# Second attention: outputs turned in 32x32 squares and divided by VectorE, score buffers fixed by head pair, a longer first table piece

## The reference

```python
proj = x @ w_in                                    # x: layer norm of the residual stream
k, v, q = split(proj, 3)                           # 16 heads of 16
scores = einsum('bhqd,bhkd->bhqk', q, k) / 4 + bias[:, q, k]   # bias depends on k - q alone
attn = einsum('bhqk,bhkd->bhqd', softmax(scores), v)
gated = attn.transpose(0, 2, 1, 3).reshape(b, s, 256) @ w_gate + b_gate
a, g = split(gated, 2)
x = x + a * sigmoid(g)
x = x + (fp8(layernorm(x)) @ w8.T + b8)
```

## Time and profile before

| | us |
|---|---|
| median of 3 runs | 2232.6 (2231.52 to 2234.2) |
| the profiled execution | 2231.65, its span 2229.9 |
| second attention, first bias sum to last division | 1567.6 to 2113.4 |
| close | 2115.8 to the end |
| mean granted TensorE clock | 0.949 |

### The profile page before, as it was taken

One profiled execution on the slowest core, in us unless ns is written; L12 is line 12 of the kernel. 1 busy time (PEld: TensorE's weight loads), 2 busy tenths in 40 slices (PEclk: granted clock), 3 DMA queues, 4 the chain that ended last, 5 costly groups with the idle time before them and its releaser, 6 DMA issues. The chain is left out here.

```text
span 2229.9 us, 38265 instructions
## 1 busy us (share of the span) xinstructions
PE 1991.4 (89%) x12467; PEld 1148.6 (52%) x12467; DVE 1164.6 (52%) x2132; ACT 1406.8 (63%) x1605; POOL 754.4 (34%) x643
## 2 busy tenths in 40 slices
PE   6899999999945799999999999778688888888797
PEld 5722333333332588888888888667122222222255
DVE  5511252524468434333333333375788888888666
ACT  5599999999732323233323332255699999999744
POOL 2000000001010423244244324110477777878622
PEclk9999999999955799999999999889799999999999
DMA  6744443435001421122022112188425343443011
GB/s 208 221 89 67 86 86 59 84 58 114 10 31 39 198 88 71 45 86 83 28 86 86 45 68 81 69 290 288 106 35 135 55 110 58 60 124 52 10 78 67
DMA packets 76840, 203.67 MB, mean 91 GB/s; under 512 B 13028, under 2 KB 28134, under 8 KB 74536
## 3 DMA queue, kind: packets, MB, share of 16 engines
q1 hardware_dynamic: 66920, 179.22, 30.4%
q0 software_dynamic: 6816, 18.62, 2.5%
q10 hardware_dynamic: 2896, 3.16, 0.5%
HBM read 338.84 MB, written 60.03 MB: 179 GB/s over the span
## 5 line engine op out<-in xcount | busy, mean ns | idle before, releaser
L1200 PE MATMUL psum<-A_qa,A_ka 50*128 50x512 f32 x2048 | 413.8, 468 | 72.5 <-ACT A1f_probs L1246 39.6
L1200 PEld LDWEIGHTS psum<-A_qa,A_ka 50*128 50x128 f32 x2048 | 170.1, 186 | 511.6 <-ACT A1f_probs L1246 257.5
L2328 PE MATMUL psum<-e_w_high,e_xT 128*128 x1136 | 386.1, 401 | 3.9 <-DVE e_xT L2278 3.8
L1358 POOL TENSOR_TENSOR A1f_probs<-A1f_probs,A1f_bias 128x512 f32<-128x512 f32 x256 | 326.3, 1285 | 154.5 <-ACT A1f_probs L1246 154.4
L1286 DVE SCALAR_TENSOR_TENSOR A1f_probs<-psum,A1f_bias 128x1024 f32<-128x1024 f32 x256 | 312.8, 1222 | 67.2 <-PE psum L1200 55.7
L1234 ACT ACTIVATE A0f_probs<-psum 128x1024 f32<-128x1024 f32 x256 | 307.8, 1202 | 23.5 <-PE psum L1200 22.2
L1246 ACT ACTIVATE A0f_probs<-psum 128x1024 f32<-128x1024 f32 x256 | 309.2, 1208 | 0.5 <-PE psum L1200 0.5
L2285 DVE TENSOR_TENSOR e_hT<-psum,e_hT 128x1024 fp32r<-128x1024 f32 x71 | 86.9, 1224 | 420.2 <-ACT e_hT L2249 420.2
L1238 ACT ACTIVATE A1f_probs<-A1f_probs 128x1024 f32<-128x1024 f32 x256 | 270.6, 1057 | 49.5 <-DVE A1f_probs L1286 49.4
L1216 PE MATMUL psum<-A1f_probs,v 128*32 128x512 f32 x2048 | 274.5, 607 | 3.7 <-POOL A1f_probs L1358 1.8
L1216 PE MATMUL psum<-A0f_probs,v 128*32 128x512 f32 x2048 | 275.0, 610 | 0.0
(11 more groups left out here) (283 smaller groups left out, 2601.0 us busy)
## 6 DMA issues: line engine op xcount, KB each, us to landing
e_w_raw<-in_experts SPq DMA_DIRECT2D x73, 3072.0 KB, 10.7
qk_parts<-L_part SPq DMA_DIRECT2D x64, 512.0 KB, 3.7
A_qa<-qk_parts SPq DMA_DIRECT2D x192, 128.0 KB, 4.3
A_ka<-qk_parts SPq DMA_DIRECT2D x192, 128.0 KB, 6.6
om<-results SPq DMA_DIRECT2D x16, 512.0 KB, 7.0
A1f_bias<-tables SPq DMA_DIRECT2D x32, 256.0 KB, 11.3
A1f_bias<-tables SPq DMA_DIRECT2D x16, 448.0 KB, 10.6
L_x<-in_x SPq DMA_DIRECT2D x8, 512.0 KB, 6.9
```

The lines of the kernel that those rows point to most:

```text
L1200: mm = e.matmul(ps[:, side * HALF:(side + 1) * HALF], self.qk.ka[rows, s, pair, kt * P:(kt + 1) * P].bitcast(FP32R), self.qk.qa[rows, s, p ...
L1358: e.tensor_tensor(fourth, fourth, self.bias_of(*w[1:], slice(self.FOURTH, GH)).rearrange("p h q -> p (h q)"), ALU.mult).then_inc(self.mult ...
L2328: mm = e.matmul(out, left[part].bitcast(FP32R), moving.bitcast(FP32R), start=start and i == 0, stop=stop and i == 2)
```

## The change

It does five things, all in the second attention and its close:

1. The block's outputs are no longer moved and turned by TensorE. `square` (VectorE) transposes a half's 128x512 sums from PSUM in 32x32 squares into `squares` and makes 16 reciprocals for each partition. `divide` (VectorE) multiplies 128x256 out of `squares`; for odd g a second 128x512 transpose in squares then puts two groups' outputs into `omT`, features in partitions. `move`, `finish` and their semaphores are gone.
2. One such piece is taken from a queue at each of the four `BY_POOL` steps of a block.
3. `BY_POOL` is now (0, 1), (0, 3), (1, 5), (1, 7), before it was (0, 0), (0, 2), (1, 4), (1, 6).
4. `score0` has a PSUM buffer of its own (one), `score1` has two. `score0` of step n waits for L1286 of step n-1, `score1` of step n for the exponential of step n-2.
5. The `FIRST` table piece has 768 columns instead of 512, and the others are waited for at (0, 3). The close reads `omT` in place of `f_omT`: its turns by TensorE and moves by ScalarE are gone, and w_gate's rows are laid out on the host in the turned order.

```diff
-    BY_POOL, THIRD_FROM, THIRD_TO = ((0, 0), (0, 2), (1, 4), (1, 6)), S - HALF, S + 2 * P
+    BY_POOL, THIRD_FROM, THIRD_TO = ((0, 1), (0, 3), (1, 5), (1, 7)), S - HALF + P, S + 3 * P
-    FIRST, OTHERS = ((S - HALF, S),), ((S, 2 * S - P), (0, S - HALF))
+    EARLY = 3
+    FIRST, OTHERS = ((S - HALF, S + (EARLY - 1) * P),), ((S + (EARLY - 1) * P, 2 * S - P), (0, S - HALF))
...
-            emptied = {"score0": self.biased[0], "score1": self.exped[1], "finish": self.normalised}
-        self.ring = Slots(3, [w for w in self.work if w[0] in emptied], emptied)
+            self.rings = [Slots(i + 1, [w for w in self.work if w[0] == kind], {kind: emptied})
+                          for i, (kind, emptied) in enumerate((("score0", self.biased[0]), ("score1", self.exped[1])))]
...
             if kt == BT - 1:
-                work.append(("move", at, half))
-                if half:
-                    todo.append(at)
+                out.extend((("square", at, half), ("divide", at, half)))
...
-                    if todo and kt == 4:
-                        work.append(("finish", todo.pop(0)))
+                    if out and (half, kt) in self.BY_POOL:
+                        work.append(out.pop(0))
...
+    def square(self, e, at, half):
+        steps = self.m.dve
+        self.wait_products(e, at, half)
+        e.wait_ge(steps.sem, steps.n)
+        e.transpose(self.squares[:, :], self.outputs(at, half)).then_inc(self.moved[half], 1)
+        e.wait_ge(self.moved[half], at + 1)
+        steps.of(e.reciprocal(self.rec[:, :], self.squares[:, :].rearrange("p (n c) -> p n c", c=32)[:, :, HD]))
+    def divide(self, e, at, half):
...
+        a = steps.of(e.tensor_tensor(self.kept(c, k, g % 2, self.spare).rearrange("p (n d) -> p n d", d=HD),
+                                     self.squares[:, :].rearrange("p (n c) -> p n c", c=32)[:, :, 0:HD],
+                                     widen(self.rec[:, :], HD), ALU.mult))
+        if g % 2:
+            e.wait_ge(steps.sem, a)
+            e.transpose(self.half_of(c, k), self.both_kept(c, k, self.spare)).then_inc(self.turned, 1)
...
 # SecondClose.pe_order
-        order = [("om", 0), ("om", 1)]
+        order = []
...
-            if u + 2 < n:
-                order.append(("om", u + 2))
...
-                mm = e.matmul(out, self.omT[:, u % 2, k, t * P:(t + 1) * P], self.wg[:, k, :], start=False,
+                mm = e.matmul(out, self.omT[:, k, at:at + P], self.wg[:, k, :], start=False,
```

More of the change, by code:

```diff
@@ L1023, in plan_second @@
     def plan_second(self):
-        work, behind, todo = [], [], []
+        work, behind, out = [], [], []
         def products():
@@ L1047, in plan_second @@
             products()
-        work += [("finish", at) for at in todo]
-        self.work = work
+        self.work = work + out
     def allocate(self, sb):
@@ L1245, in act, with wait_products @@
                 self.wait_probs(e, n)
[L1246 removed]
+                e.activation(self.probs_of(n, 1), self.buffer(w), ACT.Exp,
                              scale=SCORE_SCALE).then_inc(self.exped[1], 1)
[L1248 to L1250 removed]
             elif self.close is not None:
                 self.close.act(e, w, self.ring)
[L1254 removed]
+    def wait_products(self, e, at, half):
         e.wait_ge(self.pv_done, self.eighth(at, half, BT - 1) + 1)
[L1256 to L1260 removed]
     def shift_rows(self, e, s):
@@ L1337, in turn, with turns_before, half_of, place @@
                         self.divided[:, half, :]).then_inc(self.close.turned, 1)
+    def square(self, e, at, half):
+        steps = self.m.dve
+        self.wait_products(e, at, half)
+        e.wait_ge(steps.sem, steps.n)
[3 more added lines that the diff above has]
+    def divide(self, e, at, half):
+        steps = self.m.dve
+        g, b = self.order[at]
+        c, k = g // 2, 2 * b + half
+        e.wait_ge(steps.sem, steps.n)
+        if self.turns_before(at, half):
+            e.wait_ge(self.turned, self.turns_before(at, half))
+        a = steps.of(e.tensor_tensor(self.kept(c, k, g % 2, self.spare).rearrange("p (n d) -> p n d", d=HD),
[4 more added lines that the diff above has]
+            e.transpose(self.half_of(c, k), self.both_kept(c, k, self.spare)).then_inc(self.turned, 1)
+    def turns_before(self, at, half):
+        return sum(self.order[i // 2][0] % 2 for i in range(2 * at + half))
+    def half_of(self, c, k):
+        return self.omT.rearrange("p n d -> p (n d)")[:, c * N + k * HALF:c * N + (k + 1) * HALF]
+    def place(self, c, k, spare):
+        return self.half_of(1, k) if c == 0 else self.half_of(1, k + 1) if k + 1 < 2 * B else spare[:, :]
+    def kept(self, c, k, odd, spare):
+        return self.place(c, k, spare)[:, odd * HALF // 2:(odd + 1) * HALF // 2]
+    def both_kept(self, c, k, spare):
+        even = self.kept(c, k, 0, spare)
+        return bass.AP(tensor=even.tensor, offset=even.offset,
+                       ap=[list(even.ap[0]), [HD, HALF // 32], [HALF // 2, 2], [1, HD]])
     def pool(self, e):
@@ L2558, in act @@
         n = self.UNITS
-        for u in range(2):
-            self.move_act(e, u)
         for u in range(n + self.BEHIND):
```

166 lines of the change are left out of this document (63 added, 103 removed).

## The result

The changed kernel takes **2195.12 us** (median of 4, 2193.74 to 2198.27), the kernel before 2232.06 in the same comparison: ratio 0.9835, 95% interval 0.9818 to 0.9852. Forecast were 2189 and a gain of 43.8 us; measured are 37 us between the medians. The profiled execution took 2198.27 us, its span is 2196.5.

What follows compares the result with a forecast made beforehand. No engine is full, so the order of waits bounds the kernel. Gains of 33.6 (blocks), 4.7 (table), 1.5 (attention's end) and 4 us (close) sum to 43.8 off 2231.65, giving 2189 with the median's 0.95 added; range 2171 to 2212.

Steps and rivals of the forecast that it cites:

- Block: Second attention: a block, 33.04 us before, takes 30.2 us for even g and 31.4 for odd, mean 30.8.
- Ordinary step: Second attention: the loop between TensorE and VectorE takes 1.83 us a step, at worst 1.89, just below ScalarE's 1.87.
- Hold at (0, 1): Division at (0, 1) beside GpSimd's product, both reading SBUF: held for half a product, 0.64 us, once a block.
- GpSimd's lag: Second attention: GpSimd loses under 0.1 us a pair of products, covered by its lag; nothing, at worst 0.3 us a block.
- 15 blocks: Second attention: 2.24 us saved a block, times 15, gives 33.6 us.
- Table: Start of the second attention: VectorE's 5.15 us wait for table pieces goes; gain 4.7 us (3 to 5.5).
- End of the attention: From the last product's end to the next stage: about 3.0 us of work becomes 2.2, gain 1.5 us (0.5 to 2.5).
- Close: Closing stage: the gate product starts earlier and TensorE's turns go; gain 4 us (2 to 6.5) of 8.0 at most.
- ScalarE's pace is all that is left: Rival: slack takes in the squares, divisions are not held; block 29.9 us, time 2175; chance 0.22.
- Whole products held at each division: Rival: each division waits for a whole GpSimd product; blocks 31.8 and 33.3 us, time 2215; chance 0.14.
- Little moves: Rival: hand-over of the one score0 buffer takes 0.15 us longer; steps 1.98 us, block 32.3, time 2211; chance 0.07.
- GpSimd's queue held until empty: Slower rival: division waits for two back-to-back GpSimd products, 2.53 us; block 35.1 us, time 2253; chance 0.05.

## Why the prediction was right, and where its sizes were off

- **Block.** Forecast 30.2 and 31.4 us, measured 30.39 and 31.20; the mean (30.8, measured 30.7) was right, in part because errors met. *Ordinary step:* 1.83 forecast, 1.82 measured, and the loop of TensorE and VectorE gives it, as the run without output work shows. But VectorE's own work, for which I had 1.74, is 1.14 + 0.68 = 1.82 as well: in an ordinary step VectorE has no room. That is why work added there costs nearly its whole length (0.83 us for a square with its reciprocals, which take 0.99). *Square step:* 2.15 forecast, 2.05 measured. *Even division at (1, 5):* hidden, as forecast (a step of 1.82). *Hold at (0, 1):* 0.64 taken, 0.78 measured (1.19 - 0.41), and none at (1, 5). *Second transpose:* 0.41 over the loop at (1, 5), 0.41 measured (2.23). *Put at nothing:* "GpSimd's lag". TensorE waits for GpSimd's products at the start of every block, and that costs 0.9 us without output work (30.05 - 16 x 1.82) and 0.36 in an even block (30.39 less 12 x 1.82, 2 x 2.05, 1.82 and 2.27), a little over the 0.3 I had as the worst; in an odd block (31.20 less 12 x 1.82, 2 x 2.05, 2.23 and 3.01) nothing is left. It took the place of what the square steps came out shorter, which is luck.
- **15 blocks.** 33.6 forecast; attention without the table's part 29.4. The mean was right for blocks 1 to 13; block 14 and the second half of the first were not. In block 14 1.8 us of other GpSimd work meet the lag of the products, and the clock falls behind the wait; before, with blocks of 33 us, the longest wait of TensorE there was 0.9 us.
- **Table.** 4.7 us forecast, 4.84 measured. The step that failed is "0 to 1.5 us there, hidden by work before the barrier": the issues are not hidden. They are 1.4 us longer than in the kernel with the short piece, and the start came 1.7 us later than in the kernel before. By the medians the whole term is not measurable (2197.53 against 2197.32).
- **End of the attention.** 1.5 forecast, nothing measured from last bias sum to close, 0.6 from the last product's end (5.34 to 4.76).
- **Close.** 4 forecast, 5.5 measured: 2.2 until the first normalisation, 3.4 from there to the last. That the loop over GpSimd's root would pass on only part was right.
- **Rivals.** "ScalarE's pace is all that is left" is out as a forecast for this kernel: the slack does not take in the output work, and blocks take 30.39 and 31.20 us. As a floor it stands: without output work ScalarE is busy all of the 30.05 us, and with one hold gone blocks are 30.08 and 30.43. Whole products held at each division: held by 0.78 and at one place of two. Little moves, and GpSimd's queue held until empty: the steps of 1.82 and a hold under 0.8 exclude them.
- **What moved the work's price.** I had summed the removed and the added parts. The runs show that neither is worth much alone: against the kernel before, the old form in a light step gives 0 us a block, the old form without TensorE's transposes 0.2 at the full clock, the new form with the fixed buffers but in ordinary steps -0.1 in even groups and -1.5 in odd ones, with both divisions held. New form and light steps together give 2.2, of which 0.6 are the fixed buffers. How the other 1.6 are shared between what left ScalarE and TensorE and where VectorE's work stands is not shown: no run has the new form in the old buffers and ordinary steps without the holds.

The Trainium skill (SBUF — State Buffer, "Who interferes with whom") has VectorE with two SBUF inputs blocked wholly when it comes second behind GpSimd. The trace now agrees in that direction: 1.19 us instead of 0.41 beside products of 1.29, and 0.415 with one input in PSUM. In the rows above the division starts 0.36 us into a product, which ends at about 1800.62 (1799.33 + 1.29), and is itself done at 1800.89. That it would happen at every division, which would have given 2215, didn't come about, since at (1, 5) no product runs at that moment.

## What to carry to other kernels

Before moving work onto an engine, add up that engine's instructions in an ordinary step with their real overlaps: the same work cost 0.3 to 1.2 us a block in steps with 0.69 us of room, and the whole gain, with a second held division in it, in the others. Check there as well what runs beside it: a two-input division was 0.41 us at one place and 1.2 at another. Where a VectorE instruction would read two operands from SBUF beside GpSimd, leave one in PSUM; here that was worth 9 us more, of which 2 may be chance (block 14). And a longer transfer that is hidden may still have longer issues, on a queue that the next stage's barrier waits for.

## What the hardware showed that I had not expected

- The hold lengthens GpSimd's side as well: two products beside the held division took 2.71 us, elsewhere in this trace 2.52 to 2.54.
- SyncE's eight issues took 5.8 to 6.7 us in the kernels with the short first piece and 7.5 to 8.2 in those with the long one, though these eight move fewer bytes there.
- A wait of about 2 us on TensorE can cost twice: the wait, and then matmuls at 1.2 GHz (0.73 to 1.22 us for the scores). With ordinary steps carrying the output work the mean granted clock of one odd block fell to 0.82 and it took 39.9 us, where another with the same work took 34.5 at the full clock. In the kernel before without TensorE's transposes the clock fell in seven blocks behind waits of at most 0.8 us.
